# Two channel chunks in each step of a state-space scan, with four PSUM banks for the states and one pair of banks for B

## What is computed

```python
dt = softplus(dt_in @ dt_proj_w + dt_proj_b)
dA = exp(dt[..., None] * A)                     # A: 512 channels x 16 states
dBx = dt[..., None] * B[:, :, None, :] * x[..., None]
h = dA_t * h + dBx_t                            # over the 128 tokens of a sequence
y = sum over the 16 states of h * C_t
```

## Time and profile before

| | us |
|---|---|
| runs | 991.8, 993.68, 995.08; median 993.68 |
| profiled execution, own time | 994.63 |
| its span | 992.5 |
| TensorE busy in the span | 938.2 |
| VectorE busy | 645.1 |
| ScalarE busy | 486.3 |
| GpSimd busy | 474.4 |

### The profile page before, as it was taken

One profiled execution on the slowest core, in us unless ns is written; L12 is line 12 of the kernel. 1 busy time (PEld: TensorE's weight loads), 2 busy tenths in 40 slices (PEclk: granted clock), 3 DMA queues, 4 the chain that ended last, 5 costly groups with the idle time before them and its releaser, 6 DMA issues.

```text
span 992.5 us, 14723 instructions
## 1 busy us (share of the span) xinstructions
PE 938.2 (95%) x4648; PEld 772.2 (78%) x4648; DVE 645.1 (65%) x819; ACT 486.3 (49%) x1058; POOL 474.4 (48%) x291
## 2 busy tenths in 40 slices
PE   8996899989898989988999999999999999999998
PEld 7665677767686767766888888888888888888867
DVE  5289889999999999752454454544545444444675
ACT  4485354546354545243455545454454554545631
POOL 2112566666666666403445444554445544455422
PEclk9977999999899999999999999999999999999999
DMA  8345655655455543215744454444444444444302
GB/s 287 112 132 159 219 169 177 196 177 180 159 185 195 170 162 133 106 47 159 265 140 142 141 149 152 135 148 137 158 143 135 144 139 151 149 135 148 104 19 85
DMA packets 92315, 149.95 MB, mean 151 GB/s; under 512 B 10192, under 2 KB 34896, under 8 KB 92160
## 3 DMA queue, kind: packets, MB, share of 16 engines
q1 hardware_dynamic: 87888, 132.72, 41.7%
q10 hardware_dynamic: 4400, 16.91, 5.5%
HBM read 113.81 MB, written 35.78 MB: 151 GB/s over the span
## 4 chain that ended last, share of the span: by engine, by line
PE 61%; DVE 27%; DMA 4%; ACT 3%; issue 3%; POOL 1%; SPq 0%; DVEq 0%; ACTq 0%; POOLq 0%
DVE misc L972 11%; PE acc L378 9%; PE acc L380 8%; PE acc L379 8%; PE misc L378 6%; PE misc L380 6%; PE misc L379 6%; PE misc L580 6%; DVE w L982 6%; DVE misc L966 6%; PE misc L606 6%; PE misc L572 3%; DMA k_scratch<-kst 2%; DMA wraw<-in_wk 1%; DMA base<-in_ctxT 1%
## 5 line engine op out<-in xcount | busy, mean ns | idle before, releaser
L1136 POOL TENSOR_TENSOR y<-y,w 128x1024 f32<-128x1024 f32 x64 | 153.5, 2398 | 144.8 <-DVE w L982 144.8
L1152 POOL TENSOR_TENSOR wq_lo<-wq_raw,wq_hi 128x512 fp32r<-128x512 f32 x64 | 83.2, 1300 | 289.4 <-ACT wq_hi L801 289.4
L1063 DVE TENSOR_TENSOR ot_lo<-misc,ot_hi 128x512 fp32r<-128x512 f32 x64 | 44.3, 692 | 172.3 <-ACT ot_hi L844 172.3
L972 DVE TENSOR_TENSOR_SCAN misc<-dA,misc 128x1024 f32<-128x1024 f32 x64 | 146.9, 2296 | 10.1 <-ACT dA L666 3.3
L837 ACT ACTIVATE prob<-prob,negm 128x128 f32<-128x128 f32 x256 | 99.8, 391 | 79.4 <-DVE negm L1047 79.4
L378 PE MATMUL acc<-wv_hi,ctx_hi 128*128 128x512 f32 x256 | 108.0, 422 | 29.9 <-ACT vst L660 17.6
L378 PE MATMUL misc<-z_hi,wq_hi 128*128 128x512 f32 x256 | 106.6, 417 | 5.4 <-POOL wq_lo L1152 5.4
L826 ACT ACTIVATE q_sb<-misc 128x512 f32<-128x512 f32 x64 | 38.2, 597 | 142.9 <-PE misc L380 142.9
L378 PE MATMUL acc<-wo_hi,ot_hi 128*128 128x512 f32 x256 | 106.8, 417 | 0.0
L379 PE MATMUL acc<-wv_lo,ctx_hi 128*128 128x512 f32 x256 | 105.5, 412 | 0.0
L380 PE MATMUL acc<-wv_hi,ctx_lo 128*128 128x512 f32 x256 | 104.5, 408 | 0.0
(11 more groups left out here) (142 smaller groups left out, 1941.2 us busy)
## 6 DMA issues: line engine op xcount, KB each, us to landing
k_scratch<-kst SPq DMA_DIRECT2D x64, 256.0 KB, 2.7
bc<-xp_scratch ACTq DMA_DIRECT2D x16, 1024.0 KB, 5.9
v_scratch<-vst SPq DMA_DIRECT2D x32, 512.0 KB, 4.0
wq_raw<-in_wq SPq DMA_DIRECT2D x64, 256.0 KB, 3.3
k_sb<-k_scratch SPq DMA_DIRECT2D x64, 256.0 KB, 2.6
v_sb<-v_scratch SPq DMA_DIRECT2D x64, 256.0 KB, 2.6
wo_raw<-in_wo SPq DMA_DIRECT2D x64, 256.0 KB, 2.9
wraw<-in_wk SPq DMA_DIRECT2D x32, 256.0 KB, 4.0
```

Source lines behind the costliest of these rows:

```text
L972: dve.tensor_tensor_scan(h_ps, dA[c % 2][:, :, :].rearrange("p b s -> p (b s)"), h_ps, 0.0, ALU.mult, ALU.add).then_inc(da_free, 1)
L1136: pool.tensor_tensor(y[:, c], y[:, c], w[:, c], ALU.add).then_inc(y_ready, 1)
L1152: pool.tensor_tensor(wq_lo[p][:], wq_raw[p][:], wq_hi[p][:].bitcast(F32), ALU.subtract).then_inc(wq_lo_done, 1)
```

## The change

A step k now takes the pair of chunks 2q and 2q+1 (k = 2n + q): 32 steps of 2048 elements. `h_ps` takes all four `misc` banks. B_n keeps only the pair `acc` 2 and 3, so its copy for state n waits for the last `dbx` of state n − 1 (`dbx_done`, 2n), and it is issued after the second exponential of state n's first pair, where before it was issued after the last exponential of state n − 1. The load of B and C for state n + 1 follows that copy. `dA` has two buffers of a pair, each filled by two exponentials of one chunk, in the same places of ScalarE's queue; those of pair k wait for the scan of pair k − 2. `add_y` adds a pair. Each turn's V low part stands behind N/2 pairs, as it stood behind N steps; the K low part behind N/2 + 2 pairs, where there were N + 5 steps.

```diff
-        b_ps = [bank.rearrange("p a t -> p (a t)") for bank in (acc[:, 2:4, :], misc[:, 0:2, :])]
-        h_ps = misc[:, 2:4, :].rearrange("p a t -> p (a t)")
+        b_ps = acc[:, 2:4, :].rearrange("p a t -> p (a t)")
+        h_ps = misc[:, :, :].rearrange("p a t -> p (a t)")
-            dA = [sb(scan, f"dA{i}", [P, B, S]) for i in range(2)]
+            dA = [sb(scan, f"dA{i}", [P, 2, B, S]) for i in range(2)]
...
+            def dA_exp(k, i):
+                n, c = k // PAIRS, k % PAIRS * 2 + i
+                if k < PAIRS:
+                    act.wait_ge(sp_done, c + 1)
+                act.wait_ge(da_free, k + 1)
+                act.activation(dA[k % 2][:, i, :, 1:S], dt_[:, c].rearrange("p (b s) -> p b s", s=S)[:, :, 1:S],
...
-                if n >= 2:
-                    act.wait_ge(dbx_done, C * (n - 1))
-                act.activation(b_ps[n % 2], bc[n % TRI][:, 0], ACT.Copy).then_inc(b_ready, 1)
+                if n >= 1:
+                    act.wait_ge(dbx_done, PAIRS * n)
+                act.activation(b_ps, bc[n % TRI][:, 0], ACT.Copy).then_inc(b_ready, 1)
...
-                    dA_exp(n, c)
-                    if c == 2 and n + 2 < N:
-                        load_bc(n + 2)
-                    if c == 3 and n + 1 < N:
-                        b_copy(n + 1)
+                for e in range(done, upto):
+                    k, n = e // 2, e // (2 * PAIRS)
+                    dA_exp(k, e % 2)
+                    if n and e % (2 * PAIRS) == 1:
+                        b_copy(n)
+                        if n + 1 < N:
+                            load_bc(n + 1)
...
+            def dbx(k):
+                n, q = k // PAIRS, k % PAIRS
+                if q == 0:
+                    dve.wait_ge(b_ready, n + 1)
+                if n == 0:
+                    dve.wait_ge(u_done, 2 * q + 2)
+                if k:
+                    dve.wait_ge(prod_done, k)
+                dve.tensor_tensor(h_ps.rearrange("p (c t) -> p c t", t=T), u[:, 2 * q:2 * q + 2], two(b_ps),
+                                  ALU.mult).then_inc(dbx_done, 1)
+            def scan_step(k):
+                dve.wait_ge(da_ready, 2 * k + 2)
+                dve.wait_ge(dbx_done, k + 1)
...
-                for j in range(added, LEAD + PER * (m - 3) // 2):
-                    add_y(j)
+                for k in range(added, ADDED + PER * (m - 3) // 4):
+                    add_y(k)
```

More of the change, by code:

```diff
@@ L44 @@
 TRI = 3
-NSTEP = N * C
+PAIRS = C // 2
+NSTEP = N * PAIRS
 E = 16
@@ L54 @@
 PER = 10
+ADDED = 2
 EPS = 1e-5
@@ L671, in load_bc @@
                 if n >= TRI:
-                    act.wait_ge(prod_done, C * (n - TRI + 1))
+                    act.wait_ge(prod_done, PAIRS * (n - TRI + 1))
                     act.wait_ge(b_ready, n - TRI + 1)
@@ L680, in b_copy @@
                 act.wait_ge(bc_in[n % TRI], 16 * (n // TRI + 1))
-                if n >= 2:
-                    act.wait_ge(dbx_done, C * (n - 1))
-                act.activation(b_ps[n % 2], bc[n % TRI][:, 0], ACT.Copy).then_inc(b_ready, 1)
+                if n >= 1:
+                    act.wait_ge(dbx_done, PAIRS * n)
+                act.activation(b_ps, bc[n % TRI][:, 0], ACT.Copy).then_inc(b_ready, 1)
             def exps(done, upto):
-                for j in range(done, upto):
-                    n, c = j // C, j % C
-                    dA_exp(n, c)
-                    if c == 2 and n + 2 < N:
-                        load_bc(n + 2)
-                    if c == 3 and n + 1 < N:
-                        b_copy(n + 1)
+                for e in range(done, upto):
[5 more added lines that the diff above has]
+                            load_bc(n + 1)
                 return max(done, upto)
             def due(s):
-                return min(NSTEP, max(0, LEAD + PER * s // SPAN))
+                return min(2 * NSTEP, max(0, LEAD + PER * s // SPAN))
             for c in range(C):
@@ L936, in softplus_sum @@
                 dve.tensor_tensor(dt_[:, c], dt_[:, c], v, ALU.add).then_inc(sp_done, 1)
-            v_tile = [dA[c][:, :, :].rearrange("p b s -> p (b s)") for c in range(2)] + [bc[2][:, c] for c in range(2)]
+            v_tile = [dA[c][:, 0].rearrange("p b s -> p (b s)") for c in range(2)] + [bc[2][:, c] for c in range(2)]
             softplus_max(0)
@@ L951, in _ @@
                     dve.wait_ge(sp_done, c + 1)
-                    dve.memset(dA[c][:, :, 0:1], 0.0).then_inc(da_free, 1)
+                    for i in range(2):
+                        last = dve.memset(dA[c][:, i, :, 0:1], 0.0)
+                    last.then_inc(da_free, 1)
             for c in range(C):
@@ L955, in _, with two @@
                 dve.tensor_tensor(u[:, c], dt_[:, c], y[:, c], ALU.mult).then_inc(u_done, 1)
-            def dbx(n, c):
-                j = C * n + c
-                if c == 0:
+            def two(t):
+                return t.unsqueeze(1).to_broadcast([P, 2, T])
+            def dbx(k):
+                n, q = k // PAIRS, k % PAIRS
+                if q == 0:
                     dve.wait_ge(b_ready, n + 1)
                 if n == 0:
[L963 to L972, removed]
+                    dve.wait_ge(u_done, 2 * q + 2)
[3 more added lines that the diff above has]
+                                  ALU.mult).then_inc(dbx_done, 1)
@@ L973, in scan_step, with times_c @@
+            def scan_step(k):
+                dve.wait_ge(da_ready, 2 * k + 2)
+                dve.wait_ge(dbx_done, k + 1)
+                dve.tensor_tensor_scan(h_ps, dA[k % 2][:, :, :, :].rearrange("p c b s -> p (c b s)"), h_ps, 0.0,
                                        ALU.mult, ALU.add).then_inc(da_free, 1)
-            def times_c(n, c):
-                j = C * n + c
-                if c == 0:
+            def times_c(k):
+                n, q = k // PAIRS, k % PAIRS
+                if q == 0:
@@ L978, in times_c @@
                     dve.wait_ge(bc_in[n % TRI], 16 * (n // TRI + 1))
                 if n:
[L980 to L988, removed]
+                    dve.wait_ge(y_ready, k - PAIRS + 1)
@@ L991, in _ @@
+                dve.wait_ge(da_free, k + 3)
+                dve.tensor_tensor(w[:, 2 * q:2 * q + 2], h_ps.rearrange("p (c t) -> p c t", t=T),
+                                  two(bc[n % TRI][:, 1]), ALU.mult).then_inc(prod_done, 1)
+            for k in range(NSTEP):
+                dbx(k)
+                scan_step(k)
+                times_c(k)
             dve.wait_ge(x_again, 16)
@@ L1129, in low_w, with add_y @@
                 pool.tensor_tensor(lo[:], wraw[:], hi[:].bitcast(F32), ALU.subtract).then_inc(w_lo_done, 1)
[L1131 to L1136, removed]
+            def add_y(k):
+                q = k % PAIRS
+                if k < PAIRS:
+                    pool.wait_ge(y0_done, 2 * q + 2)
+                pool.wait_ge(prod_done, k + 1)
+                pool.tensor_tensor(y[:, 2 * q:2 * q + 2], y[:, 2 * q:2 * q + 2], w[:, 2 * q:2 * q + 2],
+                                   ALU.add).then_inc(y_ready, 1)
             low_w(1, wv_hi, wv_lo)
@@ L1141, in _ @@
             for m in range(3, 2 * NG):
-                for j in range(added, LEAD + PER * (m - 3) // 2):
-                    add_y(j)
-                added = LEAD + PER * (m - 3) // 2
+                for k in range(added, ADDED + PER * (m - 3) // 4):
+                    add_y(k)
+                added = ADDED + PER * (m - 3) // 4
                 low_w(m, wv_hi if m % 2 else wk_hi, wv_lo if m % 2 else wk_lo)
-            for j in range(added, NSTEP):
-                add_y(j)
+            for k in range(added, NSTEP):
+                add_y(k)
             def low_wq(g, p):
```

3 lines of the change are left out of this document (removed).

## The result

The changed kernel takes 1020.75 us (1020.16 to 1021.47), the kernel before 992.86 (the median with a fourth run, 992.03): a ratio of 1.0272, interval 1.025 to 1.0295. It is 27.9 us slower. The sign and the place were forecast, and a loss of 16.3 us.

A forecast was written before the change was run, and what follows sets the result against it. VectorE's own scan instructions were taken as the bound. 23.4 us less work, 42.7 of waiting where 5.4 were, and 2.2 for the last addition made +16.1 (+16.3 by turns): 1010 us, own range 1003 to 1018, wide range 995 to 1022.

The forecast's parts named there:

- the saving in VectorE's instructions: VectorE's scan: a pair takes 9.25 us against 9.98 for two steps, 23.4 us less if nothing makes VectorE wait.
- the later low part: GpSimd's additions: a pair addition takes 4.62 us, so each low part, and the last y, comes 2.2 us later.
- the gate: SyncE's store of K sum 4 waits for the V low part, holding ScalarE's queue; 3.4 us to spare before.
- the copy of K sum 6: ScalarE's copy, ahead of exponential N+3 in its queue, forecast 2.2 us later, at T + 13.5 instead of T + 11.3.
- T: In each turn, the end of the step whose addition is the last ahead of the V low part.
- P1's waits: VectorE at a turn's second pair, for exponential N+3 or B's copy: 6.8 us in turns 2, 4, 6; 3.5 otherwise.
- Rival 1: The scan runs free, ScalarE's exponentials and copies of B being ahead: 21.2 us less, 973; chance 0.09.
- Rival 2: In ScalarE's queue only exponentials delay VectorE, copies of B do not: +1.6 us, 995 to 996; chance 0.12.
- rival 3: Loads of B and C among the K weights' loads delay five turns, 10 to 15 us more: 1020 to 1025; chance 0.11.
- P3 needs the copy of B behind N+7: Fourth pair in turns 2, 4, 6: B's copy after exponential N+7 ends at T + 33.1, so no wait.
- a stretch at the lower clock: TensorE, after idling some 3 us behind the scan's end, might run slower: left at nothing, at most 1.5 us.
- Double-buffering: Keeping one buffer of B's copies where two were: some 24 us of VectorE's waiting put down to it.

The follow-up runs named there:

- added1: The change with each V and K low part one pair addition earlier in GpSimd's queue: 983.44 us against 994.48 for the kernel before, ratio 0.9882.
- lead6: The change with exponentials and copies of B two places earlier in ScalarE's queue: 986.45 us against 994.48 for the kernel before, ratio 0.9909.
- noload: The change without the loads of B and C for states 3 to 15 (states wrong): 1011.98 us against 994.48 for the kernel before, ratio 1.0175.
- lateload: The change with each load of B and C two exponentials later in ScalarE's queue: 1023.52 us against 994.48 for the kernel before, ratio 1.0301.
- before_oneb: The kernel before, single steps kept, with only one pair of banks for B: 997.21 us against 994.55, ratio 1.0025.
- bsbuf: The change with dbx reading B from SBUF, no copy to PSUM: 1049.87 us against 994.55 for the kernel before, ratio 1.0553.

## Why the prediction was right, and what was mis-sized

*Right.* The sign; the saving in VectorE's instructions (32 pairs whose parts take 2.30, 4.43 and 2.29, the sum's numbers); the later low part; the gate and the copy of K sum 6 at T + 13.55; P1's waits of 6.85, 6.94 and 6.86 us in even turns; 3.1 and 2.7 to 2.9 in odd ones (3.5 and 2.4 forecast); 7.2 us in turn 1 (6.0 measured). Rival 1 failed for the reason given against it, and added1 and lead6 both show that reason by taking it away. Rival 2 failed because the copy of B does stand behind the late exponential.

*How near it was.* 1020.75 lies outside the own range of 1003 to 1018. It lies in the wide range, 1.25 us from its end, and in the 1020 to 1025 of rival 3, which had a chance of 0.11. That it stayed inside is in part luck: turn 1 took 3.9 us less than forecast, for a reason that was not foreseen.

*Mis-sized.* The turns were to take 53.1 and 52.2 us; they took 56.4, 56.6 and 56.9, and 52.9 and 52.6. The step at fault is "P3 needs the copy of B behind N+7 ... in time for T + 34.6". It carried turn 6 of before over, where no load of B and C was under way beside those of the K weights (the last was issued at 350.19, the K weights from 363.67). The change puts that load behind N+3 in even turns. In turn 6 the DMA engines are then 0.94 busy from 386 to 394, and the high part starts 3.7 us later than the sum had it (3.2 and 3.4 in turns 2 and 4).

The delay did not stay at that. The copies of the first V sums stand behind the high part, TensorE stands still 2.9 to 3.4 us at the third V sum, and in the 5 us behind that its granted clock is 0.66 in all three turns (1.00 in noload). By exponential N+7 another 1.6 us are lost: in turn 6 it starts at T + 36.3, where the sum had T + 31.0 and noload has T + 31.6. Of these delays, 4.7 to 5.3 us together, 1.5 were slack; the rest is P3's wait of 3.2, 3.4 and 3.8. The prediction thought of a stretch at the lower clock only behind the end of the scan, and left it at nothing. No run separates the late weights from the gap and the clock that follow them; noload takes away the delay and the low clock, and the gap but for 0.9 us in turn 2. Three turns make 10.5 us. Noload gives 53.4 and lateload 53.2 to 53.5, close to the forecast. Rival 3 named this mechanism with 10 to 15 us in five turns; it came in three. It should have been in the sum: the row with 9.9 us at worst and the place of the load in the queue were both in hand.

*The rest of the 9 us.* Turn 1 took 52.6 us instead of 56.5. The sum had taken its stalls from before, where the copy of K sum 6 waited 5.09 us for a store, with a load of B and C issued at 109.80 ahead of it. In the change that load is issued at 105.40, the copy waits for TensorE alone, and exponential 7 starts at 115.90 instead of 118.80. That the load's place is the cause is likely, but no run tests it alone. Pair 1 ended 1.3 us later than forecast, since the scan began 1.5 us later (83.32, have 81.78). That start varies without regard to the change: 81.88 in lead6, 83.29 in added1. The odd turns were 1.0 us longer in all. 10.5 − 3.9 + 1.3 + 1.0 = 8.9, which is 429.63 − 420.7 at the last T. Between the profiled spans 0.7 us more came behind the scan.

*Double-buffering.* The advice of the Trainium skill ("Trainium Kernel Development and Optimization", Best Practices) was given 24 us. By before_oneb the single buffer alone costs 2.7. Most of the waits I put under it belong to the gate, and added1 removes those without a second buffer. Turn 1's 6.1 stay in added1: there the copy of B stands behind copies of K sums that wait for a store (5.21 us in the change). That attribution was wrong, though the sum was not hung on it.

## What to carry to other kernels

When a step is made coarser, its own saving is easy to read from the rows, and what feeds it has to be placed again: list for each instruction that feeds it the queue it stands in, what stands ahead, and the slack, in the new unit. Here 23 us of saving became a loss of 28 because the feeders kept their places or moved later, and became a gain of 22 when three numbers moved them (11 by the first alone). A gate that costs nothing now (3.4 us of slack) is the first thing to compute again, and so is every large DMA whose place in a queue changes.

## What the runs showed of the hardware that I had not expected

- An f32 product of VectorE with both inputs in SBUF and an addition of GpSimd run one after the other when they meet: 6.74 us for 2.30, or 6.62 for 4.61, by which started first (bsbuf).
- A 1 MB broadcast load issued behind three of four loads of 256 KB goes with a last landing some 3 us later: the high part of the K weights starts at T + 21.7 to 22.2 in the change's even turns and at T + 18.9 to 19.1 in noload (the last load takes 7.29 us to land in the chain above). In lateload's turns 3 and 5 it starts at T + 24.0 and 23.0, in noload's at T + 19.1.
- Late weights cost more than their delay. In the change's even turns TensorE stood still for 6.1 to 6.2 us at the first V sum and for 2.9 to 3.4 at the third, 11 us further on, and ran the first 5 us of the third at a granted clock of 0.66. In noload the second gap is 0.9 us or none and the clock there 1.00.
- The time at which the scan starts has two values, near 81.8 and near 83.3, in kernels that are the same up to there. What decides between them stays open.
